# As many expert chunks beside the second half's feed-forward as fit in 26 points, and a new order in the merged turns

## What is computed

```python
x = x + _L0_attn_ref(_layernorm(x), ...)              # encoder: 4 layers of linear attention (elu + 1) and relu FFN 128 -> 512 -> 128
x = x + _L0_xattn_ref(_layernorm(x), ctx, ctx, mask)  # cross-attention, 16 heads of 8
x = x + _L0_ffn_ref(_layernorm(x), ...)               # quantised 128 -> 512, depthwise convolution of 3 taps, silu, 512 -> 128
x = x + _L1_attn_ref(_layernorm(x), ...)              # self-attention, 16 heads, each row keeps its 64 largest scores
x = x + _L1_xattn_ref(_layernorm(x), ctx, ctx, ...)   # channel attention, 4 heads, a global and a local one
x = x + _L1_ffn_ref(_layernorm(x), ...)               # 8 experts, all summed:

    def expert_step(acc, w):
        wg, wu, wd = w
        h = jax.nn.silu(x @ wg) * (x @ wu)
        return (acc + h @ wd, None)
```

## Time and profile before

| what | value |
|---|---|
| median of 3 runs | 1509.03 us (1507.82 to 1510.85) |
| the profiled execution | 1503.95 us |
| its span in the trace | 1502.0 us |
| mean granted TensorE clock | 0.805 of full speed |
| busy: TensorE, VectorE, ScalarE, GpSimd (POOL) | 70%, 66%, 44%, 32% of the span |
| bytes moved by DMA | 41.22 MB, mean 27 GB/s |

### The profile page before, as it was taken

One profiled execution on the slowest core, in us unless ns is written; L12 is line 12 of the kernel. 1 busy time (PEld: TensorE's weight loads), 2 busy tenths in 40 slices (PEclk: granted clock), 3 DMA queues, 4 the chain that ended last, 5 costly groups with the idle time before them and its releaser, 6 DMA issues. The chain is left out here.

```text
span 1502.0 us, 16867 instructions
## 1 busy us (share of the span) xinstructions
PE 1055.0 (70%) x4698; PEld 626.8 (42%) x4698; DVE 989.8 (66%) x3078; ACT 663.2 (44%) x1751; POOL 484.4 (32%) x446
## 2 busy tenths in 40 slices
PE   3877745545667277787655545769999487998798
PEld 2766622323445155565433323334444144453333
DVE  6566678887467877775858887376666776644222
ACT  2444427532566255563127433455666255323121
POOL 4233337403345144443227305442222143101000
PEclk9899967855677577775558756799999778999899
DMA  3110010000000000000010000011211001112111
GB/s 120 29 28 19 18 47 1 1 0 1 1 13 17 13 17 13 17 2 1 1 49 1 1 0 8 1 42 43 64 57 43 21 22 42 57 63 63 49 63 49
DMA packets 34124, 41.22 MB, mean 27 GB/s; under 512 B 5280, under 2 KB 19248, under 8 KB 34032
## 3 DMA queue, kind: packets, MB, share of 16 engines
q1 hardware_dynamic: 33360, 38.21, 8.2%
q0 software_dynamic: 672, 1.98, 0.4%
HBM read 39.13 MB, written 1.05 MB: 27 GB/s over the span
## 5 line engine op out<-in xcount | busy, mean ns | idle before, releaser
L2008 DVE TENSOR_TENSOR big<-psum,qe 128x512 f32<-128x512 f32 x128 | 87.7, 687 | 211.6 <-PE psum L1528 103.7
L1045 ACT ACTIVATE qe<-psum 128x512 f32<-128x512 f32 x128 | 75.1, 596 | 199.0 <-PE psum L1519 196.5
L1509 PE MATMUL psum<-big,wexp 128*128 128x512 f32 x256 | 135.3, 612 | 0.0
L903 ACT ACTIVATE far<-far,half_far,fmul 128x128 bf16<-128x128 bf16 x256 | 103.2, 487 | 51.7 <-DVE hit L1786 51.7
L1799 DVE MAX8 near<-Wk 128x8 f32<-128x128 f32 x512 | 103.5, 276 | 1.2 <-DVE Wk L1809 0.2
L572 POOL TENSOR_SCALAR veps<-mv 128x4 f32<-128x4 f32 x34 | 8.3, 246 | 276.2 <-DVE mv L1706 276.2
L1148 PE MATMUL psum<-ident,h 128*128 128x128 f32 x176 | 38.5, 350 | 79.8 <-DVE h L1713 48.0
L661 POOL TENSOR_TENSOR Wk<-Wk,far 128x1024 f32<-128x1024 f32 x32 | 69.2, 2162 | 73.2 <-ACT far L903 73.2
L1284 PE MATMUL psum<-ctxT,kT 32*128 32x512 f32 x128 | 46.2, 802 | 55.5 <-DVEq L1875 42.0
L1528 PE MATMUL psum<-hT,wexp 128*128 128x512 f32 x128 | 70.6, 634 | 20.7 <-DVE big L2008 20.7
L1713 DVE TENSOR_SCALAR h<-xs,mv,rstd 128x128 f32<-128x128 f32 x128 | 56.5, 504 | 41.9 <-POOL rstd L574 38.7
(11 more groups left out here) (320 smaller groups left out, 2705.9 us busy)
## 6 DMA issues: line engine op xcount, KB each, us to landing
wexp<-in_mg SPq DMA_DIRECT2D x32, 256.0 KB, 2.7
wexp<-in_mu SPq DMA_DIRECT2D x32, 256.0 KB, 3.0
wexp<-in_md SPq DMA_DIRECT2D x32, 256.0 KB, 3.5
...
```

The source lines that it names most:

```text
L903: ins = act.activation(far[t][:, hd, :], far[t][:, hd, :], ACT.Identity, bias=half_far[:, 0:1], scale=fmul[t][:, hd:hd + 1])
L1045: act.activation(sg[k % 2], bank(5 + k % 2), ACT.Silu).then_inc(silu_done, 1)
L1509: pe.matmul(bank(4), wd[e % 2][:, c, :], hid[k % CH], start=(k % NCHUNK == 0), stop=(k % NCHUNK == NCHUNK - 1), skip_group_check=True).the ...
L2008: dve.tensor_tensor(hid[k % CH], bank(U_BANK[k]), sg[k % 2], ALU.mult).then_inc(hu_done, 1)
```

## The change

Three things.

**Chunks in the forward of the second half.** The points of group 0 start at 46 instead of 84 (`FIRST`). A new helper on each engine, `beside(n)`, does the next n points of group 0 out of the loop: two at the end of the merged turns, 4, 3 and 3 behind steps 1, 2 and 3 of the second `core_cross` (these twelve are group 0's channel attention), and 26 in its feed-forward, one chunk each (`EARLY` = 26): 2 ahead of the four steps, 3 in each step, 2 in each slot's second product and 4 behind each slot's projections. For these chunks the up product is always in bank 7, and the chain of buffers is another (`hid_of`, `sg_of`, `hTm`, `hp_of`, `ctxp_of`, `chv_of`, `ablk_of`). The second half's own stages get other banks so that 4 to 7 are free (`OUT_BANKS`, `FORWARD_BANKS`, `PROJECT_BANKS`, `CROSS_OUT_BANKS`); its cross outputs have one bank (6) where they had two. `load_keys(0)` and `load_keys(1)` are issued earlier. Two waits on the early chunks are added in the first turns of the loop (POOL, ACT and DVE wait for `EARLY` hidden or down products before they write into buffers that those use).

**Fewer chunks to a turn.** `CHUNK_PTS` has 7 points instead of 9, and point 1 is left out while bank 3 is held. Behind the 26 early ones, turns 7 to 18 hold 6, 6, 7, 7, 7, 5, 0, 0, 6, 7, 7 and 12 chunks, where turn 7 held none, turns 8 to 17 nine each and turn 18 eight. (Turns 13 and 14 have none because group 2 starts no earlier than before.) Group 1's channel attention is at points 84 to 95; the first chunks of the groups are at 58, 96, 180 and 228, the last chunk at 259.

**The order in the merged turns.** On PE the projections and both halves of the turned scores come ahead of `turned_maxima`, the attention's product and transposes move up, and the output product (L1379 before, L1459 now) comes ahead of the second half of the scores. ACT copies the maxima behind the exponentials and copies what was attended ahead of the second half of the scores.

The diff, cut:

```diff
 START2 = (NB - 1) * PTS
-CH_START = (START2, START2 + 18, (2 * G + 5) * PTS + 10 + (G - 4) * PTS, (3 * G + 5) * PTS + 10 + (G - 4) * PTS)
+PRE_TURN, PRE_CROSS, PRE_FORWARD = 2, (4, 3, 3), 26
+FIRST = START2 - PRE_TURN - sum(PRE_CROSS) - PRE_FORWARD
+CH_START = (FIRST, START2, (2 * G + 5) * PTS + 10 + (G - 4) * PTS, (3 * G + 5) * PTS + 10 + (G - 4) * PTS)
 X_FREE = 18
-CHUNK_PTS = (0, 1, 3, 4, 5, 6, 7, 9, 10)
+CHUNK_PTS = (0, 1, 3, 4, 6, 7, 9)
 LAG = 3
 NCHUNK = NEXP * CH
 BIG = float(2 ** 60)
...
+OUT_BANKS = ((6, 7), (6, 6))
+FORWARD_BANKS = (((0, 1, 2, 3, 0, 1, 2), (4, 5, 6, 7, 4, 5, 6)), ((0, 1, 0, 1, 0, 1, 0), (2, 3, 2, 3, 2, 3, 2)))
+PROJECT_BANKS = (((0, 2, 1, 3), (4, 6, 5, 7)), ((0, 1, 0, 1), (2, 3, 2, 3)))
+CROSS_OUT_BANKS = ((2, 3), (0, 3))
+X_BANK = (7, 3, 3, 3)
...
         t = max(t, CH_START[g] + 12)
         for _ in range(NCHUNK):
-            while t < TURNS * PTS and t % PTS not in CHUNK_PTS:
+            while START2 <= t < TURNS * PTS and (t % PTS not in CHUNK_PTS or t % PTS == 1 and any(c <= t < c + X_FREE for c in CH_START)):
...
-    return t + max(0, 2 - t % PTS) if t < TURNS * PTS else t
+    return t + max(0, 2 - t % PTS) if START2 <= t < TURNS * PTS else t
 def hidden_point(t):
+    if t < START2:
+        return t + 1
     return t if t >= TURNS * PTS else t + 2 if t % PTS < 2 else t + 1
...
-        q = 7 if in_x(t) or k % 2 else 3
+        q = 7 if t < START2 or in_x(t) or k % 2 else 3
...
+EARLY = sum(t < START2 for t in CHUNK_AT)
...
+        halves = [t[:, 8 * i:8 * i + 8, :].rearrange("p h k -> p (h k)").bitcast(F32) for t in (far[0], drop) for i in range(2)]
+        hid_of = [halves, [big[1][:, i, :] for i in range(CH)]]
+        sg_of = [[t[:, :] for t in ctxT], [t[:, :] for t in qe]]
+        hTm = [flat(xin[0]), flat(xin[1]), hT[1][:, :], flat(xb[1])]
...
+        qe4 = [t[:, :].rearrange("p (b c) -> p b c", b=G) for t in qe]
+        hp_of = [qe4[0], h[0][:, :, :], h[0][:, :, :], h[0][:, :, :]]
+        ctxp_of = [qe4[1], ctxt[0][:, :, :], ctxt[0][:, :, :], ctxt[0][:, :, :]]
+        chv_late = [xb[0][:, :, :], h[1][:, :, :]]
+        chv_of = [[t[:, :, 0:P] for t in kvs], chv_late, chv_late, chv_late]
+        ablk_late = [t[:, :, 0:P] for t in vv]
+        ablk_of = [[t[:, :, :] for t in at], ablk_late, ablk_late, ablk_late]
...
+            sp.wait_ge(q_pos, both(1, 2 * L))
+            load_keys(0)
             sp.wait_ge(at_mm, 2)
             for k in range(2):
                 load_expert(k, k)
             sp.wait_ge(ctxT_mm, nth(1, HALVES))
-            load_keys(0)
+            sp.wait_ge(c_k, 2)
+            sp.wait_ge(cT_mm, 1)
+            load_keys(1)
...
                     if b + 2 < NB:
                         spread(b + 2)
+                    if hf == 1 and b <= len(PRE_CROSS):
+                        beside(PRE_CROSS[b - 1])
+            point = [FIRST]
+            def beside(n):
+                for _ in range(n):
+                    channel(0, point[0] - CH_START[0])
+                    point[0] += 1
...
+                if b % NB < 2 and b >= NB:
+                    pool.wait_ge(hu_done, EARLY)
...
             def merged_turn(b):
                 here, old, new = 0 <= b < NB, 0 <= b - 2 < NB, 0 <= b + 1 < NB
                 step, fed = 0 <= b + 1 < STEPS, 0 <= b < STEPS
-                if 0 <= b - 1 < NB:
-                    maxima(b - 1)
                 if step:
                     attend(b + 1, "input")
                 if here:
...
                     penalties(b, range(6, 11))
                 if old:
                     exponentials(b - 2, 1)
+                if 0 <= b - 1 < NB:
+                    maxima(b - 1)
                 if fed:
                     feed(b, 0)
                 if here:
...
                     feed(b, 1)
                 if new:
                     scores_out(b + 1, 0)
-                    scores_out(b + 1, 1)
-                    signs(b + 1, range(0, 4))
                 if step:
                     attend(b + 1, "attended")
                 if new:
-                    signs(b + 1, range(4, H))
+                    scores_out(b + 1, 1)
+                    signs(b + 1, range(0, H))
                 if b == 5:
                     attended_out(0, 6)
...
                     if b == NB + 1:
                         context_queries(1)
                         attended_out(1, 6)
+                        beside(PRE_TURN)
...
+            point = [FIRST]
+            def beside(n):
+                for _ in range(n):
+                    channel(0, point[0] - CH_START[0])
+                    for k in CHUNKS_OF.get(point[0], ()):
+                        expert_chunk(k)
+                    point[0] += 1
...
-                    if a >= 2:
+                    if a >= 1 and hf == 1:
+                        pe.wait_ge(o_done, n)
+                    elif a >= 2:
                         pe.wait_ge(o_done, n - 1)
                     for q in range(4):
-                        mm = pe.matmul(bank(6 + a % 2)[32 * q:32 * q + 32, :], vv[s][:, c, 32 * q:32 * q + 32],
+                        mm = pe.matmul(bank(OUT_BANKS[hf][a % 2])[32 * q:32 * q + 32, :], vv[s][:, c, 32 * q:32 * q + 32],
                                        PT[a % 2][:, 4 * q:4 * q + 4, :].rearrange("p h k -> p (h k)"), start=True, stop=True)
...
                 step, fed = 0 <= b + 1 < STEPS, 0 <= b < STEPS
                 if step:
                     attend(b + 1, "input")
-                if before:
-                    turned_maxima(b - 1)
                 if old:
                     turned_scores(b - 2, 0)
                 if step:
...
                     feed(b, "input")
                 if old:
                     turned_scores(b - 2, 1)
+                if before:
+                    turned_maxima(b - 1)
                 if b == 6:
                     pe.wait_ge(n_x, NX_AT["project", 0])
                 if fed:
...
                     attend(b + 1, "sums")
                 if fed:
                     feed(b, 1)
+                if step:
+                    attend(b + 1, "attention")
                 if old:
                     outputs(b - 2, 2)
                     outputs(b - 2, 3)
                 if new:
                     scores(b + 1, 0)
                 if step:
-                    attend(b + 1, "attention")
+                    attend(b + 1, "attended")
                 if fed:
                     feed(b, "down")
+                if step:
+                    attend(b + 1, "output")
                 if new:
                     scores(b + 1, 1)
-                if step:
-                    attend(b + 1, "attended")
-                    attend(b + 1, "output")
                 if before:
                     settled_rows(b - 1)
...
                         attended_turned(1, 6)
                         pe.wait_ge(pv_done, nth(1, 3))
                         attended_projected(1, 7)
+                        beside(PRE_TURN)
             def channel(g, r):
...
                 first(0)
+                if hf == 1:
+                    beside(2)
                 for c in range(CH):
                     if c + 1 < CH:
                         first(c + 1)
                     for s in SL:
+                        if hf == 1:
+                            beside(1)
                         pe.wait_ge(c_conv, nth(s, hf * CH + c + 1))
                         if c >= 1:
                             pe.wait_ge(c_silu, nth(s, hf * CH + c))
-                        transposes(bank(4 * s + 3), yT[s], ident[:, :], c_yT_mm)
+                        transposes(bank(FORWARD_BANKS[hf][s][3]), yT[s], ident[:, :], c_yT_mm)
+                    if hf == 1:
+                        beside(1)
```

181 lines of the change are left out of this document (117 added, 64 removed).

## The result

The changed kernel took 1527.68 us, the median of 4 runs (1526.50 to 1528.21), against 1508.42 us for the kernel before (1497.15 to 1510.85): a ratio of 1.0141, with a 95% interval of 1.009 to 1.0193. It is slower, where 1500 us was forecast, and 5 us outside the range.

A forecast was written before the change was run, and what follows sets the result against it. It took VectorE to bound the cross-attention, TensorE the turns from 1022 us on, and no engine the merged turns or feed-forward. Terms -5 + 19 + 47 - 70 = -9 took the median from 1509.03 to 1500 us, range 1467 to 1523.

The forecast's parts named there:

- three signs named for being wrong: TensorE idle over 10 us in the forward stretch; cross-attention growing under 10 or over 26; chunkless turns over 30.
- Part 1: Merged turns: the new order gains in turns with fewer parts, little or nothing in full ones; -5 us.
- the end stays where it is: Merged turns: a full turn counted through ends as before, 38.4 against 38.37 us.
- The bound of -15: Merged turns, best case: half of VectorE's 4.07 + 2.54 us waits won in four full turns, beside the other gains.
- Part 2: Second half's cross-attention with twelve channel points beside it: VectorE, the bound, pays them in full; +19 us.
- The outputs have one bank instead of two: Cross-attention: outputs wait for VectorE's reading of those before; VectorE runs ahead in most steps, 1 us in all.
- Part 3: Second half's feed-forward with 26 chunks beside it: they fill TensorE's idle time and lengthen the stretch; +47 us.
- The term for the single bank 7: Feed-forward: 2.5 us for late expert weights and early up products in bank 7, each waiting for the previous hidden product.
- the third rival: Feed-forward chain of three engines leaves a third of idle time unused, merged turns gain nothing: +4, 1513 us; chance 0.15.
- Part 4: Loop turns of the second half, relieved of chunks and group 0's channel attention: -70 us, bounds -85 and -50.
- The rival of the turns' edges: Idle of about 2.9 us at seven turn edges drops TensorE's clock, about 3 us each: +12, 1521 us; chance 0.17.
- my row at 2.26 us: Profile row at 1301.69 in the kernel before: after 2.26 us of TensorE idle the clock stayed at 1.00.

## Why the prediction was wrong

The bound by stage was read rightly, and the forecast of faster rested on terms of both signs that nearly cancel: -9 out of +66 and -75. An error of a tenth in each decides the sign. In the traces the sum came to +23.4 instead of -9. Of these 32.4 us, 12.2 lie in the merged turns, 10.3 in the cross-attention, 5.3 in the feed-forward and 4.7 in the turns. The first two are steps that had the mechanism wrong, the last two are terms mis-sized. Of the three signs named for being wrong, two came: the cross-attention grew by over 26 us, and TensorE idled over 10 us in the forward stretch; the turns without chunks stayed under 30. Point by point:

- **Part 1, merged turns, -5: measured +7.2, the wrong sign.** The wait of 2.6 us that the new place of the maxima costs was in the working (2.91 measured). What failed is the step "the end stays where it is": it priced all products behind the wait at the durations of before. After 2.9 us of idle they ran at half clock, and three of the four full turns came out 2.6 to 3.8 us longer (the fourth 0.2), the one with the longer way 7.7. The last turn, 9.4 us shorter, hides more than half of this, and that turn moves by 8 us with the old order too: that the miss is not larger here is in part luck. (The bound of -15 was added up wrongly: half of 4.07 + 2.54 us in four turns is 13.2, and beside gains of 7 or more it makes -20. Nor does the bound of -85 for part 4 follow; its terms make -87. Neither carries the miss.)
- **Part 2, cross-attention, +19: measured +29.3.** The channel points came near the size forecast, 14.8 us between the two kernels with one bank, for 14.7 + 3.2, but not for the reasons given: they took 20.8 us of VectorE instead of 13.4 (last section), so some of it must lie in its idle time. The failed step is "The outputs have one bank instead of two", priced at "1 us in all"; even its upper bound of 1 us a step was too low. The bank costs 14.6 us alone, and in the changed kernel the scores ahead took 10.7 us back. I counted the wait of the outputs themselves and not the instruction queued behind it, the scores, for which the bound engine waits.
- **Part 3, feed-forward, +47: measured +52.3.** TensorE was busy 98.23 of 131.39 us from the last copy on, at 0.86. The conv part went as thought, chunk behind chunk without gaps. Of the 33.2 us of idle time that stayed, 19.8 stand ahead of the first chunk (at 908.62), 9.3 of them for VectorE's quantised rows; my stretch began behind them. The other 13.4 us stand behind it, where the sum allowed 2.5. The largest piece is one chunk's up product:

```profile
975.30 2.08 PE L1610 MATMUL psum<-xin,wexp 128*128 128x512 f32 x2 [6.19 <-DVE far L2106]
```

  It waits in bank 7 for the hidden product before it, which stands on VectorE behind a layer normalisation (1.58 us of waiting for POOL, then 3.13 us). The term for the single bank 7 was there and too small, and it is the chain that the third rival named. That the miss is not larger owes to the clock: 0.92 behind the first chunk, where it had been 0.65; the sum had left that to a bound.
- **Part 4, turns, -70: measured -65.3.** Turn by turn it is close, turn 14 within 1 us. Turn 13 gave 9.0 for 13.8. I had taken 23.2 us for a turn without chunks; it took 28.2, with VectorE busy 20.38 and TensorE 18.91 at 0.50. Without chunks TensorE sat at half clock, 1.2 GHz, and VectorE waited 6.13 us at the turn's end for its product of the settled rows.
- **The rival of the turns' edges** was right in mechanism at some edges, and small in size. The edges of turns 11 and 12 in the changed kernel:

```profile
1128.56 0.29 PE L1379 MATMUL psum<-identb,nparts 128*128 128x128 bf16 x1 [3.00 <-POOL nparts L733]
1128.77 2.08 PE L1364 MATMUL psum<-ctxT,kT 32*128 32x512 f32 x4
...
1163.11 0.23 PE L1379 MATMUL psum<-identb,nparts 128*128 128x128 bf16 x1 [3.00 <-POOL nparts L733]
1163.31 1.13 PE L1364 MATMUL psum<-ctxT,kT 32*128 32x512 f32 x4
```

  Both waits are 3.00 us (2.9 forecast). At turn 11 the turned scores behind it take 2.08 us, half clock. At turn 12 they take 1.13, as they did behind 2.26 us of idle: the clock stayed at 1.00. At turn 10 it fell behind 3.04 us, and at turn 9 behind 2.33. In the merged turns it fell at all five waits of 2.9 us. So the length of the wait alone does not decide, and my row at 2.26 us was no safe side. Turn 11 came to a clock of 0.90, not 1.00, and gave 1.5 us instead of 3; turns 10 to 12 together gave 3.2 less than forecast. The Trainium skill ("TensorE: Matmul & The Clock Gate", section "Why this matters for your kernels") gives the rule that long idle gaps between bursts bring the half rate back. The traces agree at eight of these nine places, which I had priced at full clock; they do not give a sharp length.

The deeper error is in what the move can win. I took 67 us of chunks out of turns and priced them mostly as TensorE's time. But groups 2 and 3 start no earlier, so the tail stays as it is, and what is won is only what the turns lose in length. The same top-k turn 13, by the chunks in it:

| chunks in turn 13 | 0 | 5 | 8 | 9 | 9, five other profiles |
|---|---|---|---|---|---|
| length, us | 28.2 | 31.0 | 37.6 | 37.2 | 38.4 to 40.1 |
| clock | 0.50 | 0.89 | 0.91 | 1.00 | 0.91 to 0.96 |

The columns are the changed kernel, the runs with five chunks and with none in the feed-forward, the kernel before, and the experiments that leave its chunks alone. Nine chunks lengthen the turn by 9.0 to 11.9 us, 1.0 to 1.3 each, and the first five by 0.6 us each: the turn is already 28 us long without them, and they also hold the clock up. Over turns 9 to 15 a chunk costs 1.6 us, in the feed-forward 1.9 to 2.1. They stood in the cheaper place before. This decides whether the move pays; the 32.4 us of the miss lie mainly in the first two points.
